# Routing of seven chunks moved into the attention's plan, with x1 kept in HBM and the third weight in another buffer

## The reference

```python
q, k, v = split(x @ Wq), split(x @ Wk), split(x @ Wv)          # 16 heads of 16
scores = q.k * scale + lam * (amp/phase features of q).(those of k) * scale
out = softmax(causal(scores)) @ v
x = layernorm(x + out @ Wo)                                     # x1 below
gating = softmax(x @ Wg + bg)                                   # 8 experts, top 2
h = silu((x @ W1[e] + b1[e]) * (x @ W3[e] + b3[e]))
mixed = sum over the 2 chosen e of gating[e] * (h @ W2[e] + b2[e])
x = layernorm(x + mixed @ Wf + bf)
```

## Time and profile before

| what | value |
|---|---|
| runs | 1898.84, 1900.16, 1901.07 us; median 1900.16 |
| the profiled execution's own time | 1903.75 us |
| its span, first to last instruction | 1902.1 us |
| last matmul of the attention, first of the experts' weights | at 1256.7 and 1403.6 us |
| mean granted TensorE clock | 0.950 |

### The profile page before, as it was taken

One profiled execution on the slowest core, in us unless ns is written; L12 is line 12 of the kernel. 1 busy time (PEld: TensorE's weight loads), 2 busy tenths in 40 slices (PEclk: granted clock), 3 DMA queues, 4 the chain that ended last, 5 costly groups with the idle time before them and its releaser, 6 DMA issues.

```text
span 1902.1 us, 28295 instructions
## 1 busy us (share of the span) xinstructions
PE 1732.0 (91%) x9130; PEld 912.9 (48%) x9131; DVE 1245.9 (66%) x2992; ACT 896.5 (47%) x1042; POOL 335.1 (18%) x468
## 2 busy tenths in 40 slices
PE   6999889999999999999999999977549999999965
PEld 3544344444444444444444444246526666666644
DVE  3688876787788778777777777026535555555536
ACT  2876765555555555555555554635302222222236
POOL 0000021121211211111112111114561111111111
PEclk9999979999999999999999998987669999999988
DMA  3464446030110210201102112046421111111144
GB/s 106 163 236 166 154 142 231 7 106 9 42 66 7 75 40 10 98 7 46 63 7 80 35 39 91 7 125 224 153 79 46 47 48 44 44 44 44 50 130 155
DMA packets 99595, 155.32 MB, mean 82 GB/s; under 512 B 10880, under 2 KB 60832, under 8 KB 99104
## 3 DMA queue, kind: packets, MB, share of 16 engines
q1 hardware_dynamic: 85088, 122.57, 19.6%
q0 software_dynamic: 14400, 31.37, 4.7%
HBM read 87.90 MB, written 65.35 MB: 81 GB/s over the span
## 4 chain that ended last, share of the span: by engine, by line
PE 70%; DVE 5%; issue 5%; DMA 4%; ACT 4%; SPq 1%; POOL 0%; ACTq 0%; DVEq 0%; POOLq 0%
PE att_ps_s L1046 22%; PE exp_ps_h L1679 13%; PE att_ps_o L1065 13%; PE att_ps_m L268 10%; PE exp_ps_y L1697 6%; DMA att_sums<-att_out_t 3%; DVE att_maxima L278 2%; ACT att_probs L1093 2%; PE exp_ps_t L1687 2%; PE route_ps_g L1251 1%; PE exp_ps_x L1668 1%; PE route_ps_y L1251 1%; DVE fin_stats L1210 1%; PE fin_ps_y L1251 0%; DVE fin_res L1900 0%
## 5 line engine op out<-in xcount | busy, mean ns | idle before, releaser
L1093 ACT ACTIVATE att_probs<-att_ps_s 128x1024 f32<-128x1024 f32 (+3 forms) x640 | 562.5, 896 | 445.4 <-PE att_ps_s L1046 437.3
L1046 PE MATMUL att_ps_s<-att_queries,att_keys 49*128 49x512 f32 (+3 forms) x2560 | 618.6, 555 | 22.6 <-ACT att_probs L1093 17.1
L278 DVE TENSOR_REDUCE att_maxima<-att_ps_m 128x1 f32<-128x512 f32 x768 | 487.2, 684 | 125.8 <-PE att_ps_m L268 121.5
L268 PE MATMUL att_ps_m<-att_keys,att_queries 48*128 48x512 f32 (+3 forms) x1280 | 480.6, 580 | 22.0 <-DVE att_maxima L278 11.7
L268 PEld LDWEIGHTS att_ps_m<-att_keys,att_queries 48*128 48x128 f32 x1280 | 191.3, 187 | 310.4 <-DVE att_maxima L278 159.7
L1046 PEld LDWEIGHTS att_ps_s<-att_queries,att_keys 49*128 49x128 f32 x2560 | 238.9, 190 | 143.2 <-ACT att_probs L1093 100.8
L281 DVE CUSTOM_DVE_ANT_0 att_ps_m<-att_ps_m,att_future 128x128 f32<-128x128 f32 (+3 forms) x512 | 241.4, 513 | 67.8 <-PE att_ps_m L268 66.8
L1065 PE MATMUL att_ps_o<-att_probs,att_values 128*32 128x512 f32 (+3 forms) x2560 | 270.8, 541 | 0.7 <-POOL att_probs L1149 0.7
L1679 PE MATMUL exp_ps_h<-keep_w,exp_rows_t 128*128 x568 | 258.3, 598 | 5.7 <-DVE exp_rows_t L1713 5.7
L1755 ACT ACTIVATE exp_hidden<-exp_product 128x512 f32<-128x512 f32 x71 | 44.8, 632 | 344.2 <-DVE exp_product L1738 344.2
L1149 POOL TENSOR_SCALAR_AFFINE_SELECT att_probs<-att_probs 128x512 f32<-128x512 f32 x128 | 83.5, 653 | 454.6 <-ACT att_probs L1093 454.5
(11 more groups left out here) (179 smaller groups left out, 1430.3 us busy)
## 6 DMA issues: line engine op xcount, KB each, us to landing
att_queries<-q_parts SPq DMA_DIRECT2D x64, 192.0 KB
att_keys<-k_parts SPq DMA_DIRECT2D x64, 192.0 KB
exp_rows<-sorted_rows SPq DMA_DIRECT2D x71, 129.0 KB, 2.3
v_rows<-pre_v_sb SPq DMA_DIRECT2D x8, 1024.0 KB, 4.5
q_parts<-pre_waves SPq DMA_DIRECT2D x16, 512.0 KB, 5.4
k_parts<-pre_waves SPq DMA_DIRECT2D x16, 512.0 KB, 6.1
att_values<-v_rows SPq DMA_DIRECT2D x32, 256.0 KB
out_parts<-att_out_t POOLq DMA_DIRECT2D x32, 256.0 KB, 5.9
```

The lines of the kernel that those rows point to most:

```text
L268: pe.matmul(bank[:, 0:width], self.queries[g % 2][half, c, r, P * q:P * q + P], self.keys[g % 2][half, k, r, 0:width], start=True, stop=Tr ...
L278: dve.tensor_reduce(to, bank[:, 0:width], AX.X, ALU.max).then_inc(self.s_mr, 1)
L1046: mm = pe.matmul(score_tile(unit, first, last)[:, e], keys[g % 2][half, k // TPC, r, P * (k % TPC):P * (k % TPC) + P].bitcast(F32), querie ...
L1093: act.activation(probs[:, step % PROBS, DUO * r:DUO * r + DUO, first:last], score_tile(unit, first, last), ACT.Exp, scale=SCALE).then_inc( ...
```

## The change

`route`'s work on the chunks becomes a class `Routing`, and its steps become events of `Plan`. A chunk can be routed once its inverse of the batch's last quad is stored: chunks 0 to 3 from quad 3 on, one per 125 us at the earliest (SPREAD), chunks 4 to 6 within quad 7, chunk 7 behind the attention. The steps take turns with the maxima in the ring of three banks; GpSimd's indirect stores are events too. SP gets the loads of the chunks behind its quad loads, and stores the normalised rows to a scratch tensor in HBM. So x1 is not in memory during the attention; GpSimd loads it back (8 DMAs of 512 KB) at the begin of the experts' stage into W3's old place, and adds bf at tiles 66 to 69 rather than before tile 0. The routing's buffers lie where W3 was; W3 is loaded in quad 7 to the even quad's place, with b2; W2, b1 and b3 (8 MB) are loaded behind the attention, two of W2's four blocks ahead of chunk 7's loads and the rest behind them.

```diff
+RING_KINDS = ("max", "turn_max", "project", "turn", "gates", "count")
+ROUTE = ([("divide",)] + [("project", t) for t in range(TPC)] + [("root",), ("scale",), ("normalise", 0), ("normalise", 1)]
+         + [("turn", k) for k in range(DK)] + [("gates",), ("exp",), ("choose",), ("count",)])
+LOADED, SPREAD, PUT_GAP, PUT = 10000, 125000, 700, 1300
@@ Plan.keep_inverse
+        if g % NQ == NQ - 1:
+            self.arrived[g // NQ * QC + c] = self.free["pe"] + LOADED
+    def route_due(self):
+        if self.routed not in self.arrived:
+            return None
+        if self.at_step:
+            return self.due
+        return max(self.due, self.arrived[self.routed], self.started + SPREAD if self.routed < QC else 0)
+    def route(self):
...
+        after, took = dict(divide=("dve", 1250), project=("dve", 800), root=("act", 1600), scale=("dve", 500), normalise=("act", 1200),
+                           turn=("act", 650), gates=("dve", 900), exp=("act", 1600), choose=("dve", 5000), count=("dve", 1200))[kind]
+        if kind in RING_KINDS:
+            ns = dict(project=920, turn=600, gates=2000, count=500)[kind]
+            due = self.matmul("all", ns, max(due, self.slot_ready(1)))
@@ Plan.made, ahead of the choice among scores, maxima, values and turned rows
+            if put is not None and put <= now:
+                self.put()
+                continue
+            if route is not None and route <= now + (EAGER if ROUTE[self.at_step][0] in RING_KINDS else 0):
+                self.route()
                 continue
@@ attend, SP, in the loop over g, behind quad g's loads
-                if g == QUADS:
-                    for to, rows in biases:
-                        sp.dma_start(to, rows).then_inc(s_bias, 16)
+                if g == NQ:
+                    routing.load(sp, 0, s_store, s_kept)
+                if NQ <= g < QUADS - 1:
+                    routing.load(sp, g - NQ + 1, s_store, s_kept)
+                    routing.keep_rows(sp, g - NQ)
+            routing.load(sp, QC, s_store, s_kept)
+            for to, rows in biases:
+                sp.dma_start(to, rows).then_inc(s_bias, 16)
+            routing.keep_rows(sp, QC - 1)
+            for i in range(QC + 1, NCH - 1):
+                routing.load(sp, i, s_store, s_kept)
+                routing.keep_rows(sp, i - 1)
+            routing.keep_rows(sp, NCH - 2)
+            sp.wait_ge(s_pv, QUADS * STEPS)
+            sp.wait_ge(s_scores, QUADS * len(UNITS))
+            for to, rows in later[:2]:
+                sp.dma_start(to, rows).then_inc(routing.s_last, 16)
+            routing.load(sp, NCH - 1, s_store, s_kept)
+            for to, rows in later[2:]:
+                sp.dma_start(to, rows).then_inc(routing.s_last, 16)
+            routing.keep_rows(sp, NCH - 1)
@@ attend, ScalarE: follows the plan's events
+                if event == "scores":
+                    exponential(*what)
+                elif event == "root":
+                    routing.root(act, *what)
+                elif event == "normalise":
+                    routing.normalise(act, *what)
...
@@ Routing
+    def load(self, sp, i, s_store, s_kept):
+        last = ((i // QC + 1) * NQ - 1) * QC + i % QC
+        if i >= 1:
+            sp.wait_ge(self.s_y, i * TPC)
+        sp.wait_ge(s_store[last % 2], 16 * (last // 2 + 1))
+        sp.wait_ge(s_kept[last % 2], 16 * (last // 2 + 1))
+        for k in range(DK):
...
+            sp.dma_start(self.a_raw[:, k], raw).then_inc(self.s_in, 16)
...
+            sp.dma_start(self.a_inv[:, k], inverse).then_inc(self.s_in, 16)
...
+    def divide(self, dve, i):
...
+        dve.wait_ge(self.s_in, 16 * 2 * DK * (i + 1))
+        dve.tensor_tensor(self.a_raw[:, :], self.a_raw[:, :], self.a_inv[:, :], ALU.mult).then_inc(self.s_at, 1)
@@ experts, GpSimd
-            for c in range(NCH):
-                x1_chunk = x1[:, c * TPC:(c + 1) * TPC, 0:D]
-                pool.tensor_tensor(x1_chunk, x1_chunk, bias_f[:, :].rearrange("p (o d) -> p o d", o=1).to_broadcast([P, TPC, D]),
-                                   ALU.add).then_inc(s_x1, 1)
-            pool.wait_ge(s_x1, NCH)
+            for c in range(NCH):
+                pool.dma_start(x1[:, c * TPC:(c + 1) * TPC], routed.kept[c]).then_inc(s_back, 16)
+            def add_bias(s, p):
+                first = SLOT_TILES - 1 - NCH // 2
+                if isinstance(s, int) and first <= s < first + NCH // 2:
...
+                    for c in (2 * (s - first), 2 * (s - first) + 1):
+                        x1_chunk = x1[:, c * TPC:(c + 1) * TPC]
+                        pool.tensor_tensor(x1_chunk, x1_chunk, bias_f[:, :].rearrange("p (o d) -> p o d", o=1).to_broadcast([P, TPC, D]),
+                                           ALU.add).then_inc(s_x1, 1)
-            pipelined(pool, SLOT_TILES, [(store, 2)], body=4)
+            pipelined(pool, SLOT_TILES, [(store, 2), (add_bias, 2)], body=4)
@@ program
-        w1, w3 = n.sb(first, "w1", [P, DK, NE, HID]), n.sb(second, "w3", [P, DK, NE, HID])
-        x1 = n.sb(Region(ODD, ODD_SIZE), "x1", [P, NT, ROW])
+        w1, w3 = n.sb(first, "w1", [P, DK, NE, HID]), n.sb(low, "w3", [P, DK, NE, HID])
+        x1 = n.sb(second, "x1", [P, NT, D])
-                         (bias_g[:, :], bg.partition_broadcast(P))] + weight_blocks(w1, W1) + weight_blocks(w3, W3)
+                         (bias_g[:, :], bg.partition_broadcast(P))] + weight_blocks(w1, W1)
...
-                  for to, rows in ((bias3, b3), (bias2, b2), (bias1, b1))]
+                  for to, rows in ((bias2, b2), (bias1, b1), (bias3, b3))]
...
+        later = weight_blocks(w2, W2) + biases[1:]
+        attended = attend(nc, block, att_small, features, quads, highest, made, out_parts, inv_rows, first_weights,
+                          weight_blocks(w3, W3) + biases[:1], later, routing)
```

More of the change, by code:

```diff
@@ L945, in load, with attend @@
                      self.rows_v[row, :, :, g % NQ * QUAD * VW:(g % NQ + 1) * QUAD * VW]).then_inc(arrived, 16)
-def attend(nc, block, small, features, quads, highest, made, out_parts, inv_rows, first_weights, biases):
+def attend(nc, block, small, features, quads, highest, made, out_parts, inv_rows, first_weights, biases, later, routing):
     plan = Plan().made()
-    last_event = max(i for i, event in enumerate(plan) if event[0] == "values")
-    late, late_kept = ([event[1] for event in plan[last_event:] if event[0] == kind] for kind in ("invert", "keep_inverse"))
-    plan = plan[:last_event + 1]
     with ExitStack() as stack:
@@ L1078, in _ @@
                     highest.turn(pe, take(), *what, ident)
+                elif event == "project":
+                    if what == [0, 0]:
+                        pe.wait_ge(s_expert, 16 * len(first_weights))
+                    routing.project(pe, take(), *what)
+                elif event == "turn":
+                    routing.turn(pe, take(), *what, ident)
+                elif event == "gates":
+                    routing.project_gates(pe, take(), *what)
+                elif event == "count":
+                    routing.count_before(pe, take(), *what)
         @block.scalar
@@ L1328, in route @@
+def route(nc, block, small, routing, loads, bf, keep, sorted_rows):
+    tile_expert, tile_in, tile_number, bias_f = keep
+    with ExitStack() as stack:
+        n = Names(nc, stack, "table")
+        made = routing.made
+        starts, reached, ones_f, tile_no = made.starts, made.reached, made.ones_f, made.tile_no
         pad_places = n.sb(small, "pad_places", [1, NE], I32)
@@ L1438, in _ @@
[L1438 to L1461 removed]
+                sp.dma_start(sorted_rows[bass.ds(first, P)], routing.zeros[:, :]).then_inc(s_padded, 16)
```

548 lines of the change are left out of this document (296 added, 252 removed).

## The result

The median goes from 1900.6 to 1951.3 us (four runs each; 1944.9 to 1955.4 after). The ratio is 1.0258, with an interval of 1.0231 to 1.0285: slower by 2.6%, where 1897 with a range of 1870 to 1926 had been forecast. The profiled run of after took 1952.0 us (span 1950.3).

A forecast was written before the change was run, and what follows sets the result against it. It took TensorE's work to bound the attention and chains of small steps the routing. -78.9 + 48.9 + 8 + 3 + 19 - 10 + 0 + 7 = -3.0 us, from the median 1900.2 to 1897, range 1870 to 1926.

The forecast's parts named there:

- The shortened stretch: From the attention's last matmul to the experts' first: falls from 146.9 to 68.0 us, minus 78.9.
- rival E: Behind the attention: the last 6 MB of expert weights come 10 us past the rows; 1907 us, chance 0.04.
- rival F: Chunk 6 is not routed before the attention's end, one more round of 11 us; 1908 us, chance 0.04.
- The moved work: Seven chunks' TensorE work inside the attention: plus 48.9 us, and plus 8 for breaks between other matmuls.
- The first wait: In quad 3, chunk 0's loads stand behind quad 4's in SP's queue; wait and slow clock, plus 19 us.
- Rivals A and B: A, the sum: 1897 us, chance 0.40. B, chunk 0's loads in time, no first wait: 1878, chance 0.28.
- VectorE: In the attention: 12 us more per chunk on an engine at 72% busy, counted as nothing.
- Rival C: Engines in order hold TensorE at each chunk (root, then `choose`, drain the ring), 3 us each: 1918 us, chance 0.21.
- ScalarE: In the attention: root and table loads reach TensorE by 0.4 us a chunk, plus 3; bounds 0 and 2.9 per chunk.
- Rival D: A table switch holds ScalarE twice its load's 1.28 us, all 14 reach TensorE: plus 18, 1915 us, chance 0.03.
- Bursts: Loads moved away from quad 1 (minus 4 us) and quad 6's end (minus 6): together minus 10, bounds -14 and +6.
- The experts: Experts' stage: 0 at its start; at its end GpSimd's adds delay the last store and stretch products, plus 7 us.

The follow-up runs named there:

- all_three_exp: all_three with the root replaced by an exponential, so that ScalarE loads no table (normalised rows differ); 1873.7 us, ratio 0.9869 to the kernel before.
- before_keep_act: The kernel before the change, with results copied out of PSUM by ScalarE and not VectorE; 1881.9 us, ratio 0.9903.
- keep_act: The kernel after the change, with results copied out of PSUM by ScalarE and not VectorE; 1918.6 us, ratio 1.0097 to the kernel before.
- two_of_three: all_three with the gates' 8 columns again, so only the later chunk 0 and ScalarE's copy; 1886.3 us, ratio 0.9934 to the kernel before.
- first40: The kernel after the change, with chunk 0's steps planned 40 us after its inverse and not 10; 1909.3 us, ratio 1.0061 to the kernel before.
- newton_root: all_three with 1 / sqrt made by VectorE in Newton rounds, without ScalarE's root and table loads; 1883.0 us, ratio 0.9924 to the kernel before.
- all_three: The kernel after the change, with chunk 0's steps 30 us later, 64 columns for the gates and results copied by ScalarE; 1887.2 us, ratio 0.9928.
- gates_wide: The kernel after the change, with gate logits made turned, by products of 512 columns (experts' choice differs); 1934.3 us, ratio 1.0157 to the kernel before.

## Why the prediction was wrong, step by step

**The shortened stretch: right.** Forecast 68.0 us, allowed 63 to 73, measured 63.3: the eight pads took 8.73 us and not 12.9. The weights were not late (rival E), and all seven chunks were routed inside (rival F).

**The moved work: right.** 49 us at full clock and 8 for the breaks. With first wait, copy and tables out of the way (all_three_exp against before_keep_act), quads 4 to 6 cost 8.7, 8.2 and 8.3 us a chunk and quad 7 7.1; the forecast's terms without ScalarE's give 8.1. The whole attention ends 65.8 us later in all_three_exp than in before_keep_act, for 57 forecast.

**The first wait: the step held, the size failed.** Rivals A and B turned on it. I had the data at 675 and nothing later than 680, the price 19 with an upper bound of 25 (from 660 to 675 are 15 us, not the 14 that the sum used). They came at 687.5. "About 669.3" for the end of the issues took 0.6 us for each from a stretch in which SP had no quad loads in front; behind them it was 678.1. "2.3 us later" came from there too: 9.5. TensorE's wait was 25.9 us, and the price with what followed in later quads 31 to 37 (keep_act to two_of_three, after to first40); VectorE's lost lead is the likely reason for the rest, not a shown one.

**VectorE: this step failed altogether.** "I count nothing" set its 12 us per chunk against 72% busy. What the rows show is a deadline: a row of maxima must be there when its chunk starts, and three times it was not (8.0 us of waits, and a fall of 5.1 us of lost clock at each); with the copy on ScalarE none was late. The term that stood at nothing is 6 to 20 us by the differences above. The late rows and their falls are shown, and so is a price of VectorE's time with the order fixed (10 us for 13.7, all_three_exp to newton_root). That its time is what makes the rows late is argued: the copy and the doubled search changed the order too, and GpSimd's queue has a part in it. Rival C said that engines in order hold TensorE at each chunk, and it came nearest, though 1951 lies far above its 1918. But it named `choose` draining the ring, at 3 us a chunk, and `choose` releases none of TensorE's waits from 330 to 1384. What the timeline shows comes later: the row that is not there when its chunk starts.

**ScalarE: mis-sized.** 3 us for seven chunks; measured 10 in the kernel after, 11 to 14 in all_three, against a bound of 2.9 us a chunk, 20. Half to seven tenths of the bound came, not the seventh that the sum took. Rival D was nearer with 18, by luck: it needed a longer hold than the loads', and the rows show the two loads and the root without a gap, 2.90 us.

**Bursts: half.** The fall and the 2.98 us wait at quad 6's end are gone, as forecast (-6). Without W3 behind its loads, quad 1 did not gain its 4 but is 1.9 us longer, with a wait of 1.90 us for maxima and a fall at 390.

**The experts: right.** Forecast +7, measured +6.3 up to the last store; one product took 2.91 us.

**The short products** stood in no step.

The growth of 126 is then: some 57 of work and breaks, 31 to 37 first wait, 6 to 20 VectorE, 10 to 14 ScalarE, 0 to 8 short products, less 4 for the bursts. These overlap, as all_three showed, so the sum (116 from the middles) is not exact.

In the end the exchange itself is nearly even: a chunk outside cost 11.9 us of latency (83.6 us for seven), inside it costs 8 to 10 us of TensorE, and the experts' end 6 to 7 us once. Chunk 0 alone costs 19.6 us of quad 3 even in all_three (142.3 against 122.7), with a wait of 3.26 us for maxima near 740 and a fall behind it; its cause stays open.

## What to carry to other kernels

An engine that hands out work through a small ring can make another wait although its busy share is about 70%: ask how far ahead its product is when it is needed before calling its idle time free. Price a DMA issue from a stretch in which the queue is as loaded as where the step will go. When a written plan makes the order, an edit to one cost moves the order too; only a pair of runs with the same order prices the engine alone. And count the slow clock behind a wait with the wait: in quads 4 to 6 it was the larger part.

## What the runs showed of the hardware

- Two forms of the same products hold TensorE for 1.92 us (16 records of 8 columns) and 1.88 us (4 of 512), but the granted clock fell to half within 4 us behind the first in four of six chunks of after, behind the second in none of gates_wide. 16 records with 64 columns took 2.00 us, 8 columns 1.95: the wider read is almost free.
- Copying 128 x 512 out of PSUM took VectorE 0.68 us (before) and ScalarE 0.59 (before_keep_act). Moving it, four times a quad, gave 18 us, the plan's new order included, to a kernel in which no engine but TensorE was over 72% busy in the attention.
- An issue of 256 KB that takes SP 0.57 us took 5.42 behind quad 4's loads, and its data landed 9.5 us after the last of the four issues.
